# Second attention: causal scores in blocks of 64 queries, five units of 1024 columns for six, and a softmax shift of one bfloat16 row

## What is computed

```python
def _expmap0_split(u):
    mink = -u[..., :1] ** 2 + jnp.sum(u[..., 1:] ** 2, axis=-1, keepdims=True)
    nomin = jnp.sqrt(jnp.maximum(mink, 1e-08))
    return jnp.cosh(nomin), jnp.sinh(nomin) * u[..., 1:] / nomin
...
tq, sq = _expmap0_split(q)
tk, sk = _expmap0_split(k)
neg_inner = jnp.einsum('bhie,bhje->bhij', tq, tk) - jnp.einsum('bhid,bhjd->bhij', sq, sk)
dist = jnp.arccosh(jnp.maximum(neg_inner, 1.0 + 1e-07))
scores = -dist ** 2 / np.sqrt(D)
scores = jnp.where(causal[None, None], scores, -jnp.inf)
attn = jax.nn.softmax(scores, axis=-1) * spike_mask
y = jnp.einsum('bhij,bhjd->bhid', attn, v)
```

## Time and profile before

| | us |
|---|---|
| median of 3 runs | 1960.05 (1958.11 to 1960.08) |
| span of the profiled execution | 1958.5 |
| PE busy | 1792.7 |
| ACT busy | 1679.3 |
| DVE busy | 1646.1 |
| POOL busy | 1079.7 |
| one pass of the main loop | 57.23 |

### The profile page before, as it was taken

The page is one execution under the profiler, slowest core; times in us unless marked ns, Lnnn a source line. Parts: engine busy times, 40 slices in busy tenths (PEclk is TensorE's granted clock), DMA queues, the critical chain, the costliest instruction groups (busy, mean ns, idle before and its releaser), DMA issues.

```text
span 1958.5 us, 51866 instructions
## 1 busy us (share of the span) xinstructions
PE 1792.7 (92%) x17922; PEld 1354.0 (69%) x17922; DVE 1646.1 (84%) x3472; ACT 1679.3 (86%) x2270; POOL 1079.7 (55%) x1208
## 2 busy tenths in 40 slices
PE   4668999999999999999999999999999999999987
PEld 2446777777777777777777777777777777777676
DVE  7788888888888888888888888888888888988884
ACT  8437988889898888989888898988889898887898
POOL 5336655556655555665555666555566655556533
PEclk9778999999999999999999999999999999999999
DMA  7332233233223322323332232333233233323110
GB/s 212 101 90 66 72 90 93 70 70 92 67 70 89 91 70 70 92 64 74 89 91 70 71 90 62 77 89 91 66 75 87 61 81 89 91 62 77 48 47 7
DMA packets 302073, 154.98 MB, mean 79 GB/s; under 512 B 14372, under 2 KB 298052, under 8 KB 302020
## 3 DMA queue, kind: packets, MB, share of 16 engines
q1 hardware_dynamic: 302020, 154.29, 31.4%
HBM read 82.41 MB, written 71.30 MB: 78 GB/s over the span
## 4 chain that ended last, share of the span: by engine, by line
issue 37%; POOL 26%; PE 22%; ACT 7%; DVE 5%; SPq 1%; POOLq 1%; DMA 0%; DVEq 0%; ACTq 0%
POOL zs L1405 11%; PE pu L2260 5%; PE pav L2114 3%; POOL prob L1392 3%; POOL prob L1398 3%; POOL xn L1330 2%; ACT zs L1692 2%; POOL prob L1394 2%; ACT zc L1693 2%; PE pav L2117 1%; PE pm L2235 1%; POOL rs L1313 1%; PE pm L2222 1%; POOL rs L1320 1%; PE pu L2091 1%
## 5 line engine op out<-in xcount | busy, mean ns | idle before, releaser
L1405 POOL TENSOR_TENSOR zs<-zc,zs 128x1024 f32<-128x1024 f32 x192 | 452.3, 2364 | 141.0 <-ACT zc L1693 141.0
L2260 PE MATMUL pu<-hid,h1t 128*128 128x256 f32 x1024 | 252.3, 390 | 0.4 <-DVE nmax L771 0.4
L2260 PE MATMUL pu<-hid,h2t 128*128 128x256 f32 x1024 | 238.5, 381 | 0.0
L1383 POOL TENSOR_TENSOR emb<-xn,w_sur 128x256 f32<-128x256 f32 x32 | 23.5, 733 | 358.2 <-PE pm L2134 358.2
L1692 ACT ACTIVATE zs<-zc,mhalf 128x1024 f32<-128x1024 f32 x192 | 218.7, 1139 | 0.4
L1693 ACT ACTIVATE zc<-zc,phalf 128x1024 f32<-128x1024 f32 x192 | 218.1, 1136 | 0.0
L2260 PEld LDWEIGHTS pu<-hid,h1t 128*128 128x128 f32 x1024 | 185.4, 191 | 40.9 <-issue 20.3
L758 DVE TENSOR_REDUCE zmin<-pu 128x4 f32<-128x1024 f32 (+1 forms) x154 | 187.7, 1219 | 23.9 <-DVE hid L976 16.9
L2260 PEld LDWEIGHTS pu<-hid,h2t 128*128 128x128 f32 x1024 | 187.1, 190 | 22.3 <-issue 0.5
L1713 ACT ACTIVATE zs<-zs 128x1024 f32<-128x1024 f32 x192 | 197.2, 1046 | 2.1 <-POOL zs L1405 2.1
L955 DVE TENSOR_SCALAR zc<-pu 128x1024 f32<-128x1024 f32 x154 | 186.7, 1212 | 0.0
(11 more groups left out here) (316 smaller groups left out, 4752.5 us busy)
## 6 DMA issues: line engine op xcount, KB each, us to landing
scr<-parts SPq DMA_DIRECT2D x256, 192.0 KB, 2.4
q_st<-scr SPq DMA_DIRECT2D x128, 256.0 KB, 3.9
scr<-parts SPq DMA_DIRECT2D x128, 128.0 KB, 2.4
k_st<-scr SPq DMA_DIRECT2D x64, 256.0 KB
k_st<-scr SPq DMA_DIRECT2D x32, 512.0 KB, 5.1
x<-in_L_attn_x SPq DMA_DIRECT2D x32, 128.0 KB, 3.3
out<-xold SPq DMA_DIRECT2D x32, 128.0 KB, 1.8
q_st<-m_t SPq DMA_DIRECT2D x128, 4.0 KB
```

The costliest lines, as they stand in the source:

```text
L1405: G.tensor_tensor(zs[:, c], zc[:, c], zs[:, c], ALU.add).then_inc(sum_done.sem, 1)
L2260: last = PE.matmul(u.ap[:, c * T:(c + 1) * T], w[:, k, c * P:(c + 1) * P], src[:, k, :], start=(k == 0), stop=(k == HC - 1))
```

## The change

The scores of the second attention are laid out in blocks of 64 queries. Units 0 and 1 hold queries 64 to 191 against keys 0 to 127 (`middle_cosh`), units 2 and 3 queries 192 to 255 against all keys, two heads on the two halves of the partitions (`late_cosh`), and unit 4 the two blocks that stand alone, queries 0 to 63 against keys 0 to 63 and queries 128 to 191 against keys 128 to 191, for all heads (`single_cosh`). Blocks in which every key is after every query are no longer computed, and there are 5 units. The single blocks of two heads lie on different partitions, so their values are stacked in an own tensor `v_both`, which DVE fills. The shift becomes one bfloat16 row: ACT's copy alone, without the low part.

```diff
+CUNITS = 5
+CCOLS = CUNITS * UNIT
+ROW_A, ROW_C, ROW_B = 0, H, 2 * H
+SHIFTS = 2 * H + HP
...
-                V.tensor_tensor(v_new[:, k, :], u.ap[:, 2 * D:3 * D], b_v1[:], ALU.add)
+                V.tensor_tensor(v_new[:, k, 0:D], u.ap[:, 2 * D:3 * D], b_v1[:], ALU.add)
+                odd = lambda a: a.rearrange("p (s e d) -> p s e d", e=2, d=HD)[:, :, 1, :]
+                V.tensor_tensor(v_new[QW:P, k, D:D + QW].rearrange("p (s d) -> p s d", d=HD), odd(u.ap[0:QW, 2 * D:3 * D]), odd(b_v1[0:QW, :]), ALU.add)
...
-            def clamp_minima(run):
-                unit(run, f"min{UNITS - 1}").wait_drained(dve)
-                V.tensor_scalar(zmin[:], zmin[:], MIN_COSH, None, ALU.max).then_inc(zmin_ready.sem, 1)
+            def clamp_minima(run, link):
+
+                unit(run, f"min{CUNITS - 1}").wait_drained(dve)
+                link(V.tensor_scalar(zmin[:], zmin[:], MIN_COSH, None, ALU.max))
+                first, single = (zmin[QW:P, row:row + H] for row in (ROW_A, ROW_C))
+                link(V.tensor_tensor(first, first, single, ALU.min))
+                V.tensor_copy(single, first).then_inc(zmin_ready.sem, 1)
...
+            def single_values(run, l):
+
+                dve.wait_ge(v1_ready.sem, v1_ready.at(l))
+                apart(dve)
+                if run.end:
+                    avuse(run, "av1").wait_full(dve)
+                V.tensor_copy(v_both[0:QW, :, :, 0:HD], v_mid[0:QW, :, 0:D].rearrange("p k (s e d) -> p k s e d", e=2, d=HD)[:, :, :, 0, :])
+                V.tensor_copy(v_both[QW:P, :, :, 16:16 + HD], v_mid[QW:P, :, D:D + QW].rearrange("p k (s d) -> p k s d", d=HD)).then_inc(vboth_ready.sem, 1)
...
-                if e:
-                    shift_lo(run, "mT1", 1, e)
...
-                if l:
-                    heads_reduced(unit(run, "min5"), 5, zblocks, ALU.min, False)
-                    clamp_cosh(run, 5)
                 if e:
                     spiked_norm(avuse(run, "avT1"), y1, link[E])
+                if l:
+                    single_values(run, l)
...
                     sum_minima(l)
-                    sum_cosh(l, 5)
...
-                    log(e, 5)
...
-                    square_log(e, 5)
...
-                    weights1(run, 5)
...
-                    root(run, l, 5)
...
+            def middle_cosh(u, n):
+
+                u.wait_free(pe)
+                for s in range(4):
+                    for e in range(2):
+                        pair, o = 4 * n + s, e * BANK + s * P
+                        PE.matmul(u.ap[:, o:o + P], q_st[1][halves[e], pair, e, QW:QW + P], k_st[1][halves[e], pair, 0:P], start=(s == 0), stop=False)
+                for e in range(2):
+                    out = u.ap[:, e * BANK:(e + 1) * BANK].rearrange("p (h k) -> p h k", k=P)[:, :, QW:P]
+                    last = PE.matmul(out, low_ident[halves[e], :], bc(cau0[halves[e]].unsqueeze(1), [QW, 4, QW]), start=False, stop=True)
+                last.then_inc(u.full, 1)
...
+            def single_cosh(u):
+
+                u.wait_free(pe)
+                apart(pe)
+                for pair in range(HP):
+                    for e in range(2):
+                        for a in range(2):
+                            o, own = e * BANK + pair * QW, slice(a * P, a * P + QW)
+                            PE.matmul(u.ap[halves[a], o:o + QW], q_st[1][halves[e], pair, e, own], k_st[1][halves[e], pair, own], start=(pair == 0), stop=False)
+                own_masked(u, lambda bank: bank.rearrange("p (h k) -> p h k", k=QW))
...
+                        if layer:
+                            PE.matmul(out(g, QW, T).rearrange("p (c q) -> p c q", q=QW), strip(0, h), prob1[:, 0:3, 8 * v + 4 * e + g], start=(e == 0), stop=False)
...
+                        if layer:
+                            PE.matmul(out(g, T - QW, T), strip(1, h), prob1[:, 3, 8 * v + 4 * e + g], start=False, stop=False)
...
+                if layer:
+                    for k in range(BLK):
+                        for g in range(4):
+                            last = PE.matmul(out(g, k * P, k * P + QW), v_both[:, k, 4 * v + g, :], prob1_both[:, 4 * v + g, k * QW:(k + 1) * QW], start=False, stop=(k == 1))
...
-                if e:
-                    squares_by_key(run, unit(run, "sub5"), e, 5)
...
-                if l:
-                    second_scores(unit(run, "min5"), 5)
```

More of the change, by code:

```diff
@@ L199, in wait_drained @@
         eng.wait_ge(self.free, self.count + 2)
-DVE_LINKS = {"norm": 2, "first": 2, "middle": 28, "last": 1, "end": 5}
+DVE_LINKS = {"norm": 2, "first": 2, "middle": 28, "last": 3, "end": 5}
 def bc(ap, shape):
@@ L1019, in iteration @@
                 if l:
-                    heads_reduced(unit(run, "min2"), 2, zblocks, ALU.min, False)
+                    minima(run, 2)
                     clamp_cosh(run, 2)
@@ L1049, in iteration @@
                 if l:
-                    heads_reduced(unit(run, "min4"), 4, zblocks, ALU.min, False)
+                    minima(run, 4)
                     importance(l, link[L])
@@ L1156, in closing @@
                 square_log(r0.end, 0)
-                shift_lo(r0, "mT1", 1, r0.end)
                 square_log(r0.end, 1)
@@ L1239, in closing @@
                 spikes(r2.end, k2[E])
-                shift_lo(r2, "mT1", 1, r2.end)
                 output(r2, r2.out)
```

371 lines of the change are left out of this document (195 added, 176 removed), and 6 rows, old and new, of the table CLOSING_USES.

## The result

The changed kernel takes 1995.22 us (median; 1991.03 to 2001.37) where the kernel before took 1959.2 in the same session: ratio 1.0186, 95% interval 1.0166 to 1.0207. It is slower by 1.9%, where I had forecast 1935 us and 1.3% faster.

A forecast was written before the change was run, and what follows sets the result against it. Four stretches of a pass, set by ACT, DVE's path, PE, and DVE level with PE, sum to -0.57 us, -15.4 over 27 passes; closing -10 and opening +1 give 1935 us, range 1917 to 1957.

The forecast's parts named there:

- S1: Stretch of a pass from `embT` to `y1`, 12.57 us, set by ACT; forecast to change by 0.
- This cover: PE's wait for ACT in the stretch from `embT`: attention may grow by 0.75 us before `avT1` is late.
- S4: Stretch from `qkv1` to the next `embT`, DVE and PE level; two added DVE instructions, forecast +0.08 us.
- the 0.25 that I had named as a sign of being wrong: Forecast's sign of failure: a small instruction on DVE takes over 0.25 us.
- rival C: DVE's small instructions cost more, at 0.35 us each 1969 us, slower; 0.11 together with slower for another reason.
- S2: Stretch from `y1` to `exp0`, 13.52 us; DVE's added work +0.72, ACT's earlier arrival at `mT` -0.67: +0.05 us.
- S3: Stretch from `exp0` over layer 0's attention to `qkv1`, set by PE; mainly the wait for POOL's masks goes: -0.70 us.
- rival B: Small matmuls have a floor: the single unit takes 1.28 us instead of 0.56, time 1955 us; chance 0.11.
- Rival A: PE is the bound, every removed PE instruction counts, about 3.3 us a pass, 1862 us; 0.13 with its half-way case.
- The rest of the run: Mainly the closing, where ACT is nearly full and loses sixth-unit work: -10 us, bounds -5 and -14.
- the opening: Start of the run, which gets clears of `v_both` on ACT and `v_new` on DVE: +1 us, bounds 0 and 2.

The follow-up runs named there:

- run 3: Changed kernel with four idle TensorE transposes ahead of `embT`, whose result `embT` overwrites: 1953.35 us, 0.9958 of the kernel before.
- run 4: Changed kernel with DVE's two copies into `v_both` ahead of the norm and four idle transposes ahead of `embT`: 1952.92 us, 0.995 of the kernel before.
- Run 5: run 4 with the copies made as reductions and DVE's two extra additions in the embedding's chain gone: 1919.37 us, 0.9794 of the kernel before.
- run 6: Run 5 with the last quarter of the second layer's hidden product moved ahead of `max5` on PE: 1938.09 us, 0.9879 of the kernel before.
- run 12: Run 5 with two idle transposes in place of four: 1919.51 us, 0.978 of the kernel before.
- run 2: Changed kernel with DVE's two copies into `v_both` made as reductions, in their old place: 1959.38 us, 0.9986 of the kernel before.
- run 10: Run 5 without the idle transposes: 1927.02 us, 0.9817 of the kernel before.

## Why the prediction was wrong

**The step that failed** is in S1: "All of this only lengthens PE's wait for `o_t` ... S1 changes by 0. This cover stands whatever the matmuls cost"; and likewise in S4: "The 1.41 us turn into a new wait of PE at `embT`", at no price. Most waits came as forecast: 1.12 us ahead of `embT` (1 to 1.5 forecast), 0.37 ahead of the attention and 0.71 ahead of `avT1` at full clock (1.2 forecast for the last two together), and DVE waited 2.82 us for `avT1` (2.8 forecast). One was not in the forecast, 0.65 us ahead of `max1`, for ACT's `prob`. What I took for free was not. With these waits the clock fell in 23 of 27 passes, and with two or four idle transposes in them in none (runs 3 to 6 and 12); where it fell behind `embT`, at the lower clock the attention took 3.78 us (1022.57 to 1026.35) in place of 2.33 (1082.03 to 1084.36); that used up the cover, and `single_values` behind it fell into POOL's sum. I listed no rival on the clock, although the forecast itself made PE idle for 2 us where it had been busy. In numbers: 38.5 us over the 27 passes, of the 46.8 by which I missed them (forecast -15.4, measured +31.4).

**S4**, +0.08 forecast, +0.59 measured: "I take 0.16, bounds 0.08 and 0.28" for an addition. It was 0.32, above my upper bound and over the 0.25 that I had named as a sign of being wrong, and the change of partitions was the reason. The chain's head grew by 0.74, and 0.17 of it went into the 0.30 us by which PE had followed DVE (0.13 now). Run 5 gave 0.68 back. This is rival C's mechanism in one of its two stretches: its point of balance was 0.25, but its price, 1969, was still 26 us short of the result.

**S2**, +0.05 forecast, -0.02 measured. The path was right: `max5` now waits 0.58 us for DVE and starts 1.24 behind `y1` (0.64 before), `mT` 3.53 (3.11), and ACT, which had come to its copy of `mT` 0.89 behind the start of `mT`, now waits for it and comes 0.41 behind. The size of DVE's part, 0.69 from L756 to `max3` where I had 0.72, was luck. The two small instructions on the minima cost 0.53 of it, and the copies, 0.58 long, nothing, because `rk_m` behind them ends 0.28 us behind the end of POOL's sum with or without them (before, in the changed kernel, in run 4):

```profile
1021.24 1.10 DVE L791 TENSOR_TENSOR rk_m<-rk_t,lat_rows 32x256 f32<-32x256 f32 x1
```

```profile
1091.53 0.44 DVE L806 TENSOR_TENSOR rk_m<-rk_t,lat_rows 32x256 f32<-32x256 f32 x1
```

```profile
1074.43 1.10 DVE L806 TENSOR_TENSOR rk_m<-rk_t,lat_rows 32x256 f32<-32x256 f32 x1
```

The sums end at 1022.06, 1091.69 and 1075.25. This is also why S2 stays at 13.50 in run 4, where the copies have left the chain.

**S3**, -0.70 forecast, -0.84 measured. The wait for POOL's masks is gone. The 32 matmuls of the single unit take 0.27 us in all, and 0.59 with the mask, where I had forecast 0.56:

```profile
1069.48 0.44 PE L2081 MATMUL pu<-k_st,q_st 64*64 64x64 bf16 x32
1069.75 0.39 PE L2089 MATMUL pu<-cau,ident_bf 64*64 64x512 bf16 x4
1070.07 0.44 PE L2191 MATMUL pm<-ident,xn 128*128 128x128 f32 x2
```

That is 8 or 9 ns each, so rival B is out. My estimate of 0.8 us from the 60 cycles that the Trainium skill gives each matmul (TensorEngine Tiling (Array Packing), Instruction Overhead) had put them one behind the other. The matmuls take the four tiles in turn, and on one tile they come every 34 ns, above the 25 ns of that estimate, so the rows do not contradict the 60 cycles for a single tile; they show that these do not add up over four.

**S1 at full clock**, 0 forecast, +0.04 measured: the attention's 2.33 us are the 2.31 that I had worked out from columns. Rival A, PE as the bound, is out as well: run 3 gave PE 0.87 us more work in each pass and the time fell by 2%, and the wait at `exp0` grew (0.84 to 1.08) where A would have shrunk it.

**The rest of the run**, -10 forecast with bounds of -5 and -14, measured -0.7. The three pairs of copies, five of the six held, and a clock of 0.96 ate most of it: with reductions it is -5.6 (run 2), and with the additions gone too -4.2 to -8.0 (runs 5, 6, 10 and 12). For the opening (+1 forecast) no run shows a cost: its end is 0.9 us later in this execution, less than it differs between executions.

The undisturbed pass alone (-0.27 by the means) with the rest as in run 2 and the opening would have given about 1959 - 7 - 6 + 1 = 1947, inside my range of 1917 to 1957. So the count of the work was fair, though a pass gained only half of what I forecast even then, and what it set off on PE's clock and on DVE beside POOL was missing.

## What to carry to other kernels

When a change turns TensorE's work into waits, ask what its clock will do, not only who hides the wait: a rival for it belongs in every forecast that lengthens a wait, and a few idle transposes in the wait are a cheap test of it. Price a small VectorE instruction by its partitions and form, not by its size: output in another partition group costs both seams, and a copy from SBUF to SBUF may stand for the whole length of a GpSimd instruction. Read passes one by one before means: 57.0, 57.4, 59.5 and 60.8 told what 58.4 hid.
